# Marks of a routing table, compared on VectorE eight sets at a time instead of set by set on GpSimd

## Chip, cores and metric

One core of one Trainium2 chip runs the whole kernel. The metric is device time in microseconds from start to end of one execution; lower is better. The kernel is a single launch, so what lies between launches does not count.

## What is computed

The reference is a small transformer layer over 32 sequences of 128 tokens (4096 tokens, width 512), in float32. The first two parts (a token embedding with a low-rank correction and a norm over the whole table of 32,000 rows; an attention with quantised weights and activations) are not touched here. The third part is:

```python
h = h + ffn(layernorm(h))
# ffn(x): 8 routed experts of width 352, each token goes to its best K = 2; one shared expert of width 704
shared_out = (silu(x @ Wsg.T) * (x @ Wsu.T)) @ Wsd.T
scores = softmax(x @ Wr.T)
topk_scores, topk_idx = top_k(scores, 2)
w_full = sum over k of one_hot(topk_idx, 8) * topk_scores
out_e = (silu(x @ Wg[e].T) * (x @ Wu[e].T)) @ Wd[e].T
routed_out = sum over e of out_e * w_full[e]
return routed_out + shared_out
```

## The kernel before, in words

`experts` (line 1041 on) computes this third part. It works in blocks of 256 tokens. The first 16 blocks (kind A, numbers 0 to 15) put all tokens through one half of the shared expert; then come 39 routed blocks (32 full ones of kind B, 7 half ones of kind H), which each take the tokens of one expert; then 16 more blocks (kind C) do the other half of the shared expert. On each engine the order of the blocks is written out by hand in `each_block`: blocks 0 to 3, then a loop over blocks 4 to 11 (two per turn), then 12 to 15, and so on. The engines are coupled by semaphores alone.

One block n, in the order that each engine issues it:

- TensorE (PE) does `up_full(n)`: gate and up projections into three PSUM tiles `up_ps`, j = 0, 1, 2, each float32 product as three passes over a high and a low part (L1642 to L1644, L1671 to L1676). Then it does `down(n-1)`, the down projection of the block before, into `down_ps`. Before `up_full(n)` it waits for the low part `xT_lo` of block n; before it overwrites `up_ps` j it waits until VectorE has read tile j of block n-1 (`h_done`); before `down(n-1)` it waits for `h_lo` of block n-1.
- VectorE (DVE) does `turned_lo(n+1)`, the low part of the next block's input (L1419, 128x1024); `gate_full(n)`: for j = 0, 1, 2 the product h (L1554, and L1558 to L1565 for j = 2) and, once ScalarE has rounded it to `h_hi`, the rest `h_lo` (L1567); then `take_y(n-1)`, which adds two down results into H (L1538).
- ScalarE (ACT) rounds the next input (`xT_hi`, L1339), does silu on each `up_ps` tile (L1357 to L1361) and rounds h (L1365).
- GpSimd (POOL) is not part of a shared block. Its work in this stage is the slot table, below.

The slot table. Each of the 8192 (token, choice) pairs gets a slot, that is a place in some routed block. VectorE plans this in three pieces laid between the shared blocks: `plan_blocks` behind block 0, `plan_experts` behind block 1, `plan_slots` behind block 3 (L1486 to L1516). `plan_slots` ends with, for each of the SETS = 64 sets of 128 pairs (32 sequences times 2 choices), the slot's tile number `tile_f` (0 to 70; SLOT_TILES = 71) and its row `row_f` in that tile (0 to 127). The inverse table, which token sits in each slot, is then made by matrix products: `at_row` has a 1 where a pair's row number equals the column (128 columns a set), `at_tile` has, where the tile number equals the column (71 columns), the sequence number i in its first half and the lane number in its second. Both are bf16 in one tile `slot_marks`. TensorE's `sum_table` adds 64 products at_row x at_tile (L1637) into `route_ps`. It stands in TensorE's order between blocks 11 and 12. VectorE's `read_table` (L1522, L1524) turns the sums into the list `slot_tokens`, behind block 12 in its own order. GpSimd then gathers the rows of the routed blocks with indirect DMAs (L1316) into the buffers `xr`, the first for block 16 once `xT_lo` of block 14 is done.

The marks are made by GpSimd in a loop over the 64 sets, three instructions a set, L1302 to L1304 (see the diff); the third adds one to `slots_marked`, and `sum_table` waits for `slots_marked` set by set. GpSimd starts them when `plan_slots` has ended (semaphore `plan`). The instruction that ends `plan_slots` is L1516.

`slot_marks` lies in the space of the second weight buffer, `w_split[1]`; ScalarE writes there for the first routed block during block 15, and waits for `table_summed` before. The SyncE queue (SP) loads the tokens' rows for each shared block (two buffers, paced by `xT_lo`), and the weights of the first routed block as soon as its expert is known, before `plan_slots`.

Of the kernel before, what the change touches and what calls it, by code (L numbers as in the profile page):

```python
# [20 lines left out]
ALU = mybir.AluOpType  # L21
# [3 lines left out]
P = 128  # L25
SEQS, T = 32, 128
# [7 lines left out]
EXPERTS, TOP = 8, 2  # L34
# [1006 lines left out]
def experts(nc, packed, w_stage, x2_dram, x2T_dram, y_dram, out, H, ident, ones, gate_values, gate_experts):  # L1041
# [6 lines left out]
    with ExitStack() as ctx:  # L1048
        def sb(name, shape, dt=F32):
            return ctx.enter_context(nc.sbuf_tensor(name, shape, dt))  # L1050
# [7 lines left out]
        SETS = TOP * SEQS  # L1058
        w_split = [sb("w_split0", [P, 2 * PACKED], F32R)]

        with nc.sbuf_tensor("slot_marks", [P, SETS * (P + 2 * SLOT_TILES)], BF16) as slot_marks:
            at_row = slot_marks[:, 0:SETS * P].rearrange("p (n c) -> p n c", n=SETS)
            at_tile = slot_marks[:, SETS * P:].rearrange("p (n c) -> p n c", n=SETS)
# [26 lines left out]
        slot_i = sb("slot_i", [P, TOP * SEQS], I32)  # L1090
        lane = sb("lane", [P, 1])
        row_no = sb("row_no", [P, P])
        slot_tokens = sb("slot_tokens", [P, SLOT_TILES], I32)
        block_expert = sb("block_expert", [P, ROUTED_BLOCKS], I32)

# [33 lines left out]
        route_ps = ps("route_ps", [P, 512])  # L1129

        made, masked, plan, counted, blocks_known = sem("made"), sem("masked"), sem("plan"), sem("counted"), sem("blocks_known")
        slots_marked, table_summed, table_lo_out, table_made = sem("slots_marked"), sem("table_summed"), sem("table_lo_out"), sem("table_made")
        stage_in = [sem(f"stage_in{i}") for i in range(3)]
        w_hi_done = [sem(f"w_hi_done{i}") for i in range(3)]
        w_lo_done = [sem(f"w_lo_done{i}") for i in range(3)]
# [53 lines left out]
        def w_buffer(odd, kind):  # L1189
            return (odd + 1) % 2 if kind in ("B", "H") else 0  # L1190

        def each_block(eng, body, after_first=None, after_second=None, after_fourth=None, before_twelfth=None, after_twelfth=None):

            body(0, 0, "A", None, "A")
            if after_first:
                after_first()
            body(1, 1, "A", "A", "A")
            if after_second:
                after_second()
            body(2, 0, "A", "A", "A")  # L1200
            body(3, 1, "A", "A", "A")
            if after_fourth:
                after_fourth()
            with eng.Fori(0, (B_FROM - 8) // 2) as m:
                for u in range(2):
                    body(m * 2 + (4 + u), u, "A", "A", "A")
            if before_twelfth:
                before_twelfth()
            body(B_FROM - 4, 0, "A", "A", "A")
            if after_twelfth:  # L1210
                after_twelfth()
            body(B_FROM - 3, 1, "A", "A", "A")
            body(B_FROM - 2, 0, "A", "A", "A")
            body(B_FROM - 1, 1, "A", "A", "B")
            for n in range(B_FROM, C_FROM + 1):
                body(n, n % 2, kind_of(n), kind_of(n - 1), kind_of(n + 1))
            with eng.Fori(0, (SHARED_BLOCKS - 2) // 2) as m:
                for u in range(2):
                    body(m * 2 + (C_FROM + 1 + u), u % 2, "C", "C", "C")
            body(N - 1, 0, "C", "C", None)  # L1220
# [61 lines left out]
        def _(pool):  # L1282
# [11 lines left out]
            pool.affine_select(out=below[:, :], in_=below[:, :], compare_op=ALU.is_gt, fill=0.0, base=0, pattern=[[1, P]],  # L1294
                               channel_multiplier=-1).then_inc(masked, 1)

            pool.wait_ge(made, 6)
            pool.wait_ge(plan, 1)
            for t in range(TOP):
                for i in range(SEQS):  # L1300
                    n = t * SEQS + i
                    pool.tensor_scalar(at_row[:, n, :], row_no[:, :], row_f[:, 0, n:n + 1], None, ALU.is_equal)  # L1302
                    pool.tensor_scalar(at_tile[:, n, 0:SLOT_TILES], row_no[:, 0:SLOT_TILES], tile_f[:, 0, n:n + 1], float(i), ALU.is_equal, ALU.mult)  # L1303
                    pool.tensor_scalar(at_tile[:, n, SLOT_TILES:], row_no[:, 0:SLOT_TILES], tile_f[:, 0, n:n + 1], lane[:, 0:1],  # L1304
                                       ALU.is_equal, ALU.mult).then_inc(slots_marked, 1)
            pool.wait_ge(table_made, 1)
            for r in range(ROUTED_BLOCKS):
                n = B_FROM + r
# [106 lines left out]
        def _(dve):  # L1415
# [69 lines left out]
            def plan_slots():  # L1485
# [23 lines left out]
                for t in range(TOP):  # L1509
# [6 lines left out]
                dve.scalar_tensor_tensor(out=row_f[:, 0, :], in0=tile_f[:, 0, :], scalar=float(-P), in1=slot_f[:, 0, :],  # L1516
                                         op0=ALU.mult, op1=ALU.add).then_inc(plan, 1)

            def read_table():

                dve.wait_ge(table_summed, 1)
                dve.tensor_copy(table_lo[:, 0, :], route_ps[:, SLOT_TILES:2 * SLOT_TILES]).then_inc(table_lo_out, 1)  # L1522
                dve.wait_ge(table_lo_out, 1)
                dve.scalar_tensor_tensor(out=slot_tokens[:, :], in0=route_ps[:, 0:SLOT_TILES], scalar=float(P), in1=table_lo[:, 0, :],  # L1524
                                         op0=ALU.mult, op1=ALU.add).then_inc(table_made, 1)

# [88 lines left out]
            turned_lo(0, 0, "A")  # L1615
            weights_lo(0, 2, 0)
            plan_choices()
            each_block(dve, body, plan_blocks, plan_experts, plan_slots, None, read_table)
            take_y(N - 1, "C")
            dve.wait_ge(y_taken, 2 * N)  # L1620
            for i in range(SEQS - 2, SEQS):
# [3 lines left out]
        def _(pe):  # L1625
# [7 lines left out]
            def sum_table():  # L1633

                for n in range(SETS):
                    pe.wait_ge(slots_marked, n + 1)
                    mm = pe.matmul(route_ps[:, 0:2 * SLOT_TILES], at_row[:, n, :], at_tile[:, n, :], start=(n == 0), stop=(n == SETS - 1))  # L1637
                mm.then_inc(table_summed, 1)

# [179 lines left out]
```

## Time and profile before

| | us |
|---|---|
| median of 3 runs | 1592.19 |
| lowest and highest of them | 1588.05, 1597.53 |
| the profiled execution, its own time | 1594.22 |
| its span in the trace, first to last instruction | 1592.5 |
| mean granted TensorE clock, share of full speed | 0.979 |

The profile gives busy times of each engine, also in 40 slices of the span, so that a slice is 39.8 us. A group is a set of instructions of one line, engine and shape; behind its busy time stands the idle time of the engine just before it and what ended it. "Busy" on TensorE is modelled by the profiler, so the spacing of starts is the better measure there. The granted clock is given as a share of the higher of TensorE's two levels (2.4 GHz; 0.5 is the lower, 1.2 GHz).

### The profile page before, as it was taken

What the parts mean: (1) busy time and instruction counts of PE and PEld (TensorE: products, weight loads), DVE (VectorE), ACT (ScalarE), POOL (GpSimd) and SP (SyncE); (2) the same over time, 40 slices, a digit from 0 to 9 for tenths busy, and PEclk for the clock granted to TensorE, in tenths of its full rate; (3) what the DMA queues carried; (4) which work ended last, traced back from release to release, by engine and by line L of the source; (5) the groups of instructions that cost most, each with busy time, mean ns of one, the idle gap of its engine ahead of it and who ended that gap; (6) DMA issues with size and microseconds to landing.
All of it is one profiled execution on the core that took longest, in us unless ns stands there. A gap on an engine that the chain in (4) does not pass through costs nothing.

```text
span 1592.5 us, 36456 instructions
## 1 busy us (share of the span) xinstructions
PE 1406.5 (88%) x13322; PEld 1181.4 (74%) x13386; DVE 1175.7 (74%) x2334; ACT 909.7 (57%) x1692; POOL 551.8 (35%) x701
## 2 busy tenths in 40 slices
PE   4566875999999998699938999999999999999997
PEld 2233333777777776599918999898898898999996
DVE  5598986888888986575513777778777787767776
ACT  3787873777777776333302566666566665633331
POOL 4454545445454420019992121111111110034433
PEclk9999999999999999799968999999999999999999
DMA  8999985222222211131100477777877777443465
GB/s 305 353 327 287 329 277 108 59 72 71 68 75 65 66 41 55 67 109 52 40 14 27 152 230 270 268 241 242 282 242 265 256 236 269 168 159 126 144 209 194
DMA packets 76013, 271.45 MB, mean 170 GB/s; under 512 B 10321, under 2 KB 10833, under 8 KB 71681
## 3 DMA queue, kind: packets, MB, share of 16 engines
q1 hardware_dynamic: 59472, 226.03, 41.2%
q0 software_dynamic: 16432, 44.05, 10.9%
q8 instruction: 59, 0.97, 0.2%
q14 instruction: 50, 0.40, 0.1%
HBM read 226.27 MB, written 43.78 MB: 170 GB/s over the span
## 4 chain that ended last, share of the span: by engine, by line
PE 22%; DVE 11%; issue 8%; POOL 8%; ACT 7%; DMA 2%; SPq 0%; ACTq 0%; POOLq 0%; DVEq 0%
PE up_ps L1642 4%; PE up_ps L1644 4%; PE up_ps L1643 4%; ACT w_split L1343 3%; DVE w_split L1428 3%; POOL slot_marks L1302 3%; POOL slot_marks L1304 3%; POOL slot_marks L1303 2%; PE down_ps L1643 2%; PE down_ps L1644 2%; PE down_ps L1642 2%; DVE xT_lo L1419 2%; DVE h L1554 1%; DMA slot_rows<-y_rows 1%; PE up_ps L1676 1%
## 5 line engine op out<-in xcount | busy, mean ns | idle before, releaser
L1642 PE MATMUL up_ps<-xT_hi,w_split 128*128 128x256 f32 x1280 | 367.3, 287 | 15.2 <-DVE xT_lo L1419 8.2
L1643 PE MATMUL up_ps<-xT_lo,w_split 128*128 128x256 f32 x1280 | 363.6, 284 | 0.0
L1644 PE MATMUL up_ps<-xT_hi,w_split 128*128 128x256 f32 x1280 | 363.6, 284 | 0.0
L1642 PEld LDWEIGHTS up_ps<-xT_hi,w_split 128*128 128x128 f32 x1280 | 246.6, 193 | 18.0 <-DVE xT_lo L1419 8.3
L1643 PEld LDWEIGHTS up_ps<-xT_lo,w_split 128*128 128x128 f32 x1280 | 246.8, 193 | 1.4
L1644 PEld LDWEIGHTS up_ps<-xT_hi,w_split 128*128 128x128 f32 x1280 | 246.6, 193 | 0.0
L1365 ACT ACTIVATE h_hi<-h 128x256 fp32r<-128x256 f32 (+1 forms) x192 | 80.2, 418 | 258.2 <-DVE h L1554 195.9
L1316 POOL DMA_INDIRECT xr<-x_rows,slot_tokens x71 | 71.5, 1008 | 417.9 <-PE xT_ps L1737 381.4
L393 PE MATMUL norm_ps<-a_split,b_split 96*128 96x500 f32 x256 | 140.1, 685 | 55.9 <-DVE W L294 31.6
L294 DVE TENSOR_TENSOR W<-W,norm_ps 128x1000 f32<-128x1000 f32 x128 | 146.9, 1188 | 39.6 <-PE norm_ps L393 33.8
L1343 ACT ACTIVATE w_split<-w_stage 128x1408 fp32r<-128x1408 f32 (+1 forms) x123 | 169.1, 1411 | 3.9 <-PE down_ps L1644 1.8
L1642 PE MATMUL down_ps<-w_split,h_hi 128*128 128x512 f32 (+1 forms) x405 | 159.1, 393 | 1.5 <-DVE H L1538 1.5
L1644 PE MATMUL down_ps<-w_split,h_lo 128*128 128x512 f32 (+1 forms) x405 | 160.2, 396 | 0.0
L1643 PE MATMUL down_ps<-w_split,h_hi 128*128 128x512 f32 (+1 forms) x405 | 160.1, 395 | 0.0
L393 PEld LDWEIGHTS norm_ps<-a_split,b_split 96*128 96x128 f32 x256 | 68.4, 315 | 120.2 <-DVE W L294 82.9
L1357 ACT ACTIVATE act_g<-up_ps 128x256 f32<-128x256 f32 (+1 forms) x192 | 71.5, 372 | 140.8 <-PE up_ps L1644 122.4
L1567 DVE TENSOR_TENSOR h_lo<-h,h_hi 128x256 fp32r<-128x256 f32 (+1 forms) x192 | 82.0, 427 | 93.8 <-ACT h_hi L1365 91.4
L232 ACT ACTIVATE W<-W 128x1000 f32<-128x1000 f32 x128 | 131.3, 1026 | 32.5 <-DVE W L294 31.9
L1324 POOL DMA_INDIRECT comb<-slot_rows,slot_i x64 | 75.8, 1184 | 178.1 <-DVE H L1546 97.1
L1428 DVE TENSOR_TENSOR w_split<-w_stage,w_split 128x1280 fp32r<-128x1280 f32 x82 | 121.6, 1483 | 2.0 <-ACT w_split L1343 1.9
L186 POOL TENSOR_TENSOR a_split<-a_f,a_split 32x1000 fp32r<-32x1000 f32 x32 | 74.0, 2314 | 117.7 <-ACT a_split L224 105.5
L1554 DVE TENSOR_TENSOR h<-act_g,up_ps 128x256 f32<-128x256 f32 x128 | 53.2, 415 | 72.1 <-ACT act_g L1357 72.1
(278 smaller groups left out, 3182.4 us busy)
## 6 DMA issues: line engine op xcount, KB each, us to landing
W<-table_c SPq DMA_DIRECT2D x32, 2000.0 KB
w_stage<-packed SPq DMA_DIRECT2D x80, 704.0 KB
w_stage<-packed SPq DMA_DIRECT2D x40, 768.0 KB
xr<-x_turned SPq DMA_DIRECT2D x32, 512.0 KB
slot_rows<-y_rows SPq DMA_DIRECT2D x32, 512.0 KB
x_rows<-x SPq DMA_DIRECT2D x32, 256.0 KB, 2.0
x_turned<-x2T SPq DMA_DIRECT2D x32, 256.0 KB, 3.9
out<-H SPq DMA_DIRECT2D x32, 256.0 KB
```

What stands on the lines that cost most here:

```text
L186: pool.tensor_tensor(a_split[c % 4][64:96, :], a_f[0:32, c % 4, :], a_split[c % 4][0:32, :].bitcast(F32), ALU.subtract).then_inc(a_lo, 1)
L232: act.activation(W[:, q, k, :], W[:, q, k, :], ACT.Square, accum_out=part[:, q % 2, k:k + 1]).then_inc(squared, 1)
L294: dve.tensor_tensor(w, w, norm_ps[k % 2][:, :, 0:HALF], ALU.add).then_inc(added, 1)
L393: mm = pe.matmul(norm_ps[k % 2][:, h, 0:HALF], b_split[:, k * P:(k + 1) * P], a_split[q][:, h * HALF:(h + 1) * HALF], start=True, stop=True)
L1324: pool.indirect_dma_start(out=comb[i % 2][:, t, :], out_offset=None, in_=y_dram, in_offset=bass.IndirectOffsetOnAxis(ap=slot_i[:, t * SEQS ...
L1343: act.activation(hi_part(piece, buffer), staged(piece), ACT.Copy).then_inc(w_hi_done[piece], 1)
L1365: act.activation(h_hi[odd][0:f, j, :], h[0:f, j, :], ACT.Copy).then_inc(h_hi_done, 1)
L1428: dve.tensor_tensor(up_lo[buffer][:, k, :], whole[:, :, 0:BOTH_FROM], hi[:, :, 0:BOTH_FROM], ALU.subtract).then_inc(w_lo_done[piece], 1)
L1567: dve.tensor_tensor(h_lo[odd][0:f, j, :], h[0:f, j, :], h_hi[odd][0:f, j, :].bitcast(F32), ALU.subtract).then_inc(h_lo_done, 1)
L1642: pe.matmul(out, a_hi, b_hi, start=first, stop=False)
L1643: pe.matmul(out, a_hi, b_lo, start=False, stop=False)
L1644: return pe.matmul(out, a_lo, b_hi, start=False, stop=last)
```

## The change

The comparisons move to VectorE. `mark_slots(g)` runs ahead of block 4 + g on VectorE (g = 0 to 7, `in_loop` of `each_block`) and compares eight sets in one instruction for `at_tile` (128x568) and one for `at_row` (128x1024), both with operands that are broadcast by access pattern. GpSimd keeps two multiplications for each eight sets, 128x568 each: marks times the sequence number into the first half, marks times the lane number in place in the second half. It waits for both comparisons of the group before them, and for its own first product before the second. TensorE waits once for each eight sets. GpSimd makes one more small constant, `seq_no`. A semaphore in `read_table` is replaced by the common counter of VectorE's plan (`did`).

```diff
+        MARKED = 8
+        MARK_BLOCKS = SETS // MARKED
...
+        seq_no = sb("seq_no", [P, SETS])
...
         def each_block(eng, body, ..., in_loop=None, before_twelfth=None, after_twelfth=None):
...
-            with eng.Fori(0, (B_FROM - 8) // 2) as m:
+            with eng.Fori(0, MARK_BLOCKS // 2) as m:
                 for u in range(2):
+                    if in_loop:
+                        in_loop(m * 2 + u)
                     body(m * 2 + (4 + u), u, "A", "A", "A")
...
         # GpSimd
-            pool.wait_ge(made, 6)
-            pool.wait_ge(plan, 1)
-            for t in range(TOP):
-                for i in range(SEQS):
-                    n = t * SEQS + i
-                    pool.tensor_scalar(at_row[:, n, :], row_no[:, :], row_f[:, 0, n:n + 1], None, ALU.is_equal)
-                    pool.tensor_scalar(at_tile[:, n, 0:SLOT_TILES], row_no[:, 0:SLOT_TILES], tile_f[:, 0, n:n + 1], float(i), ALU.is_equal, ALU.mult)
-                    pool.tensor_scalar(at_tile[:, n, SLOT_TILES:], row_no[:, 0:SLOT_TILES], tile_f[:, 0, n:n + 1], lane[:, 0:1],
-                                       ALU.is_equal, ALU.mult).then_inc(slots_marked, 1)
+            pool.iota(seq_no[:, :].rearrange("p (t i) -> p t i", t=TOP), pattern=[[0, TOP], [1, SEQS]], base=0, channel_multiplier=0,
+                      allow_small_or_imprecise_dtypes=True).then_inc(made, 1)
+            pool.wait_ge(made, 7)
+            for g in range(MARK_BLOCKS):
+                n = slice(g * MARKED, (g + 1) * MARKED)
+                pool.wait_ge(slots_marked, (g + 1) * 2)
+                mark = at_tile[:, n, SLOT_TILES:]
+                pool.tensor_tensor(at_tile[:, n, 0:SLOT_TILES], mark, seq_no[:, n].unsqueeze(2).to_broadcast([P, MARKED, SLOT_TILES]),
+                                   ALU.mult).then_inc(tokens_marked, 1)
+                pool.wait_ge(tokens_marked, g * 2 + 1)
+                pool.tensor_tensor(mark, mark, lane[:, 0:1].unsqueeze(2).to_broadcast([P, MARKED, SLOT_TILES]), ALU.mult).then_inc(tokens_marked, 1)
...
         # VectorE
+            def mark_slots(g):
+                if not isinstance(g, int):
+                    dve.wait_ge(plan, 1)
+                n = bass.ds(g * MARKED, MARKED)
+                rows = row_no[:, :].unsqueeze(1)
+                dve.tensor_tensor(at_tile[:, n, SLOT_TILES:], rows[:, :, 0:SLOT_TILES].to_broadcast([P, MARKED, SLOT_TILES]),
+                                  tile_f[:, 0, n].unsqueeze(2).to_broadcast([P, MARKED, SLOT_TILES]), ALU.is_equal).then_inc(slots_marked, 1)
+                dve.tensor_tensor(at_row[:, n, :], rows.to_broadcast([P, MARKED, P]), row_f[:, 0, n].unsqueeze(2).to_broadcast([P, MARKED, P]),
+                                  ALU.is_equal).then_inc(slots_marked, 1)
...
             def read_table():
                 dve.wait_ge(table_summed, 1)
-                dve.tensor_copy(table_lo[:, 0, :], route_ps[:, SLOT_TILES:2 * SLOT_TILES]).then_inc(table_lo_out, 1)
-                dve.wait_ge(table_lo_out, 1)
+                did(dve.tensor_copy(table_lo[:, 0, :], route_ps[:, SLOT_TILES:2 * SLOT_TILES]))
...
-            each_block(dve, body, plan_blocks, plan_experts, plan_slots, None, read_table)
+            each_block(dve, body, plan_blocks, plan_experts, plan_slots, mark_slots, None, read_table)
...
         # TensorE, sum_table
                 for n in range(SETS):
-                    pe.wait_ge(slots_marked, n + 1)
+                    if n % MARKED == 0:
+                        pe.wait_ge(tokens_marked, (n // MARKED + 1) * 2)
```

## Rows read from the trace of the kernel before

**Rows 1.** The page: busy time, share of the span, instructions.

```profile
PE 1406.5 (88%) x13322; PEld 1181.4 (74%) x13386; DVE 1175.7 (74%) x2334; ACT 909.7 (57%) x1692; POOL 551.8 (35%) x701
```

**Rows 2.** The page: busy tenths and granted clock in 40 slices.

```profile
PE   4566875999999998699938999999999999999997
...
PEclk9999999999999999799968999999999999999999
```

**Rows 3.** Windows: stretch, its length, busy us of each engine, clock, DMA share, GB/s.

```profile
714.00:726.40 12.40, 12.40 (x88) 11.59 (x87) 8.99 (x20) 6.22 (x15) 11.93 (x19) 1.00 0.23 85
787.80:800.30 12.50, 12.50 (x88) 11.50 (x86) 6.73 (x14) 4.48 (x10) 11.55 (x19) 1.00 0.14 43
800.30:842.00 41.70, 9.03 (x66) 4.95 (x65) 2.25 (x3) 0.21 (x1) 37.98 (x65) 0.60 0.04 13
```

**Rows 4.** Tile slot_marks: duration ns min/median/max, first and last start, and waits.

```profile
L1302 POOL TENSOR_SCALAR slot_marks<-row_no,y_rows x64: 602/609/1615, 711.7 to 839.8; 128x128 bf16<-128x128 f32 x64
...
L1304 POOL TENSOR_SCALAR slot_marks<-row_no,y_rows,lane x64: 608/613/1252, 713.9 to 841.1; 128x71 bf16<-128x71 f32 x64
```

**Rows 5.** Timeline of PE: start us, duration us, idle before and its releaser.

```profile
701.85 0.28 PE L1642 MATMUL up_ps<-xT_hi,w_split 128*128 128x256 f32 x1
...
714.17 0.28 PE L1642 MATMUL up_ps<-xT_hi,w_split 128*128 128x256 f32 x1
...
800.36 2.90 PE L1637 MATMUL route_ps<-slot_marks 128*128 128x142 bf16 x43
...
839.85 0.30 PE L1637 MATMUL route_ps<-slot_marks 128*128 128x142 bf16 x1 [1.60 <-POOL slot_marks L1304]
...
841.96 0.55 PE L1642 MATMUL up_ps<-xT_hi,w_split 128*128 128x256 f32 x1
...
856.15 0.28 PE L1642 MATMUL up_ps<-xT_hi,w_split 128*128 128x256 f32 x1
```

**Rows 6.** Timeline of DVE, from the end of the plan on.

```profile
711.30 0.23 DVE L1516 SCALAR_TENSOR_TENSOR y_rows<-y_rows 128x64 f32<-128x64 f32 x1
711.60 1.23 DVE L1419 TENSOR_TENSOR xT_lo<-xr,xT_hi 128x1024 fp32r<-128x1024 f32 x1
712.75 0.41 DVE L1554 TENSOR_TENSOR h<-act_g,up_ps 128x256 f32<-128x256 f32 x1
...
719.75 1.22 DVE L1419 TENSOR_TENSOR xT_lo<-xr,xT_hi 128x1024 fp32r<-128x1024 f32 x1
...
779.43 0.42 DVE L1554 TENSOR_TENSOR h<-act_g,up_ps 128x256 f32<-128x256 f32 x1 [1.53 <-ACT act_g L1357]
...
789.11 1.22 DVE L1419 TENSOR_TENSOR xT_lo<-xr,xT_hi 128x1024 fp32r<-128x1024 f32 x1
```

**Rows 7.** Groups of DVE by shape: busy us, mean ns, idle before.

```profile
L1419 DVE TENSOR_TENSOR xT_lo<-xr,xT_hi 128x1024 fp32r<-128x1024 f32 x32 | 39.4, 1231 | 11.6 <-PE up_ps L1676 6.9 <-ACT xT_hi L1339 4.6
...
L1506 DVE TENSOR_TENSOR comb<-comb,y_rows 128x256 f32<-128x256 f32 x1 | 0.4, 425 | 0.0
```

**Rows 8.** Lines of POOL, its multiplications: duration ns min/median/max, first and last start.

```profile
L601 POOL TENSOR_TENSOR diag_t<-ident,dequant x32: 398/399/401, 261.2 to 603.9; 128x128 f32<-128x128 f32 x32
...
L596 POOL TENSOR_TENSOR H<-H,S_bc x32: 1263/1852/1871, 255.2 to 574.8; 128x512 f32<-128x512 f32 x32
...
L186 POOL TENSOR_TENSOR a_split<-a_f,a_split x32: 2286/2312/2343, 14.6 to 231.2; 32x1000 fp32r<-32x1000 f32 x32
```

**Rows 9.** Line 307 of DVE: duration ns min/median/max, and its register instructions.

```profile
L307 DVE TENSOR_SCALAR a_group<-a_rows x8: 242/780/1835, 31.1 to 232.2; 128x128 f32<-128x128 f32 x4, 128x128 f32 x4
L307 DVEq FUSED_REGOPS  x4: 65/65/65, 152.9 to 230.9; - x4
```

**Rows 10.** Timelines of POOL and DVE where a long POOL product meets L307.

```profile
29.36 2.29 POOL L186 TENSOR_TENSOR a_split<-a_f,a_split 32x1000 fp32r<-32x1000 f32 x1 [0.42 <-ACT a_split L224]
...
31.05 0.68 DVE L307 TENSOR_SCALAR a_group<-a_rows 128x128 f32<-128x128 f32 x1 [2.65 <-DMA a_rows<-lora_a_t,rows_i]
```

More of the change, by code:

```diff
@@ L1131, in experts @@
         made, masked, plan, counted, blocks_known = sem("made"), sem("masked"), sem("plan"), sem("counted"), sem("blocks_known")
-        slots_marked, table_summed, table_lo_out, table_made = sem("slots_marked"), sem("table_summed"), sem("table_lo_out"), sem("table_made")
+        slots_marked, tokens_marked, table_summed, table_made = sem("slots_marked"), sem("tokens_marked"), sem("table_summed"), sem("table_made")
         stage_in = [sem(f"stage_in{i}") for i in range(3)]
@@ L1190, in w_buffer, with each_block @@
             return (odd + 1) % 2 if kind in ("B", "H") else 0
-        def each_block(eng, body, after_first=None, after_second=None, after_fourth=None, before_twelfth=None, after_twelfth=None):
+        def each_block(eng, body, after_first=None, after_second=None, after_fourth=None, in_loop=None, before_twelfth=None, after_twelfth=None):
             body(0, 0, "A", None, "A")
```

## Prediction

> **What bounds the kernel now.** I read the totals first. TensorE is busy for 88% of the span, VectorE for 74%, GpSimd for 35% [rows 1]: GpSimd looks harmless. The 40 slices say where TensorE is not busy. After its slow first stage it stands at 9 almost everywhere, except in slices 17 and 21 (counted from 1), and the granted clock falls in the same two [rows 2]. Slice 21 is 796 to 836 us. The windows around it show what happens [rows 3]: until 800.3 us TensorE has no idle time at full clock, then for 41.7 us it is busy for 9.0, at a mean clock of 0.60, while GpSimd is busy for 38.0 of them and VectorE, ScalarE and DMA do almost nothing (DMA share 0.04).
>
> The tile that GpSimd works on is `slot_marks`: 64 sets of three instructions, from 711.7 us to 841.1 [rows 4]. It cannot start earlier, since the plan ends at 711.5 [rows 6]. TensorE comes to `sum_table` at 800.36, finds 43 sets ready and takes them in 2.90 us, and then waits for GpSimd set by set, one each 1.90 us, until block 12 begins at 841.96 [rows 5]. So in this stage GpSimd ends last, and in the shared blocks before it TensorE does. One block takes TensorE 714.17 - 701.85 = 12.32 us [rows 5].
>
> **What is removed.** Of the 41.60 us between 800.36 and 841.96 the 64 products themselves remain. The 43 ready ones took 2.90 us including a tail of about 0.2 for the last one to drain, so 0.064 us each, 4.1 us for 64. That leaves 41.6 - 4.1 = **37.5 us** of waiting. There is a second part. Block 12 takes from 841.96 to 856.15 [rows 5], 14.19 us where another takes 12.32: the mean clock in the wait was 0.60 and block 12 starts at the lower one. Without the wait the clock should stay at 1.00, as in both full blocks of [rows 3]: **1.9 us** more.
>
> **What is added on VectorE.** Both comparisons read two SBUF operands and are float32 in. The nearest rows are float32 `tensor_tensor` instructions: 1024 elements in 1.231 us (1.22 when nothing disturbs, as at 789.11 in [rows 6]) and, with a broadcast second operand, 256 in 0.425 [rows 7]. The line through them is 1.04 ns an element and 0.16 fixed. That makes 1.22 us for `at_row` and 0.16 + 568 x 1.04 ns = 0.75 for `at_tile`, together **1.97 us a block** and 15.8 in all. The bf16 output and the broadcast of both operands have no row of their own; I take the plain rate since the broadcast in L1506 cost nothing.
>
> Is it on the path? VectorE needs 719.75 - 711.60 = 8.15 us for a block when it waits for nothing but ScalarE's roundings [rows 6], and TensorE needs 12.32. So there is room for about 4.2 us a block, and in the settled blocks VectorE waits 1.5 us for silu at tile 0 alone (the row at 779.43 in [rows 6]) and is busy for 6.7 of 12.5 [rows 3]. Work of 1.97 fits there, and there I cost it at nothing; what hides it is TensorE's own 12.32. If VectorE's block passed that, each further us would cost a us, eight times.
>
> It does not fit in block 4. VectorE comes out of the plan late: its `turned_lo(5)` starts at 711.60 and the product for tile 0 of block 4 ends at 712.75 + 0.41 = 713.16, and TensorE needs both for block 5, which it begins at 714.17 [rows 5, 6]. The slack is 1.0 us. `mark_slots(0)` stands ahead of both: 1.97, plus a wait for the plan's last instruction and a few register instructions for the moving slices, at 0.065 each [rows 9], about 0.3 together. TensorE then stands for 2.3 - 1.0 = **1.3 us**, once. The other conditions have more room (low part of h and tile 2 are over 2 us early), and after that VectorE gains on TensorE by 12.3 - 10.4 = 1.9 a block, so block 6 is no longer late.
>
> **What is left on GpSimd.** Two multiplications of 568 elements for each group. Its products have rows at 128, 512 and 1000 elements: 0.399, 1.263 at least, 2.312 [rows 8]; by a straight line 568 take 1.39 us. Two are 2.8 us in each block of 12.3. The pessimistic end is L596's median, 1.852 for 512, which gives some 2.05 us each. The last group is marked ahead of block 11, on VectorE around 791 us, so GpSimd is done at 795 to 797, and TensorE asks at 800.4 + 1.3. The margin is at least 4 us, and TensorE's 8 waits in `sum_table` cost nothing. The new `seq_no` is one short constant before the plan, in a time when GpSimd is idle. `read_table` does the same work with another semaphore: nothing.
>
> **GpSimd against VectorE.** A long GpSimd product can hold VectorE up. In [rows 10] L186 runs from 29.36 to 31.65; L307 on VectorE starts at 31.05 and ends at 31.73, 0.68 us for work that takes 0.242 alone, and its longest is 1.835 [rows 9]. In the stage at hand L1302's longest is 1.615 against a median of 0.609 [rows 4], so it goes the other way too. Before the change GpSimd's instructions were short; now they are 1.4 us long. What VectorE may lose is at most the two products, 2.8 us a block, part of it in gaps where it waits for ScalarE anyhow. I expect about 1 us a block, hidden from block 5 on, and nothing at block 4's critical start, because `turned_lo` is issued directly behind the comparison that GpSimd waits for. The bounds: 0, and 1.4 us at the start plus (8.15 + 2.3 + 2.8 - 12.3) = 0.95 in each of the seven later blocks, 8 us.
>
> The Trainium skill (SBUF — State Buffer, section "Who interferes with whom") speaks against the change here: it says that a VectorE instruction with two SBUF inputs and a GpSimd instruction that reads SBUF exclude each other, and that the one that comes second blocks until the first has ended. Taken literally every comparison, L1419 and L1567 could wait for a full product, which is the upper bound just named and the first rival below. The trace agrees in the form of [rows 10].
>
> **The sum.** Removed: 37.5 + 1.9 = 39.4. Added: 1.3. Net 38.1. Against the profiled execution's own time, 1594.2 - 38.1 = 1556.1. That execution lies 2.0 above the median of the three runs, so for the median I say 1592.2 - 38.1 = **1554.1 us**. What follows block 12 moves as a whole: nothing is loaded during the stall that a later stage lives on (DMA share 0.04), and the gathers for the routed blocks wait for `xT_lo` of block 14, which moves along.
>
> **Rivals.**
>
> 1. *GpSimd's products block VectorE for their whole length, block after block.* For it: [rows 9, 10]. Against it: VectorE's block has gaps, and its products with PSUM operands are most of the rest. The gain shrinks by up to 8 us: 1554 + 8 = 1562. Faster still. Chance 0.13.
> 2. *The wait comes back in another place.* VectorE reaches the mark ahead of block 11 late, or GpSimd's products run much slower on bf16 operands with two broadcasts, so that TensorE waits in `sum_table` for the last groups. It decides when GpSimd needs more than 12.3 us a group, 4.4 times what I price. At 17 us a group it would end at 712 + 8 x 17 = 848, 6 us later than now: about 1592 + 6 - 4 = 1594, no change. Chance 0.02.
> 3. *Slower: the comparisons run at a slow rate and VectorE bounds blocks 4 to 11.* The place is `mark_slots`; the price is the slowest rate that the trace has for VectorE, L307's longest, 1.835 us for 128 elements [rows 9], 14 ns an element; that is 23 us for 1592 elements, at half that 11.4. The point from which it decides against the change: 8 x (8.15 + m - 12.3) > 38, that is m over 8.9 us a block, 4.5 times my price. At m = 11.4 it costs 8 x 7.25 = 58 and the kernel ends near 1612. Against it: L1506, a broadcast at full rate. Chance 0.03.
> 4. *The change doesn't do what it says*: the start of the routed blocks is held by something else that the stall hid, such as the first gathers, and the gain is given back in part. The nearest thing is the idle DMA in [rows 3], which speaks against it. Half of the 38 would leave 1573. Chance 0.04.
>
> The forecast itself has 0.78.
>
> **How the numbers follow.** Three runs of the kernel before span 1588 to 1598, so the best case is 39.4 gained without the stall at block 5 and 5 for the runs: 1548. The other end is rival 1 with 8 us and 4 for the runs: 1566. That leaves out rivals 2 to 4 and some tails. About 0.5% (8 us) is what a measurement of this kernel can tell from no change. Faster by more than that: forecast, rival 1 and rival 4, 0.95. Within it: rival 2, 0.02. Slower: rival 3, 0.03.
>
> **What the profile of the changed kernel would show.** `sum_table` as one run of 64 products in about 4 us, near 801.7, with no GpSimd behind it as releaser, and block 12 near 806 at clock 1.00. Two comparisons in each of eight blocks on VectorE, 0.75 and 1.22. One idle stretch of TensorE of 1.3 us before block 5, released by `xT_lo` or h. GpSimd with 16 products of 1.4 us. L1419 and L1567 longer than 1.22 and 0.42 in these blocks would show the blocking; idle time of TensorE at several blocks with VectorE as releaser would make rival 1 or 3 true. I am wrong if the time is outside 1548 to 1566, or if the stages before 700 or after 870 change their length.

## The result, and the profile of the changed kernel

| | before | changed |
|---|---|---|
| median of the runs, us | 1593.41 (4 runs) | 1555.70 (4 runs, 1555.41 to 1556.17) |
| ratio, 95% interval | | 0.9765 (0.9743 to 0.9786) |
| span of the profiled execution, us | 1592.5 | 1553.7 |
| mean granted clock | 0.979 | 0.991 |

The change is worth 37.7 us, 2.4%, and the median of 1555.70 stands against a forecast of 1554.1 us. That forecast was 38.1 below 1592.19, the median of the kernel before over three runs; with a fourth run it is 1593.41. The page's totals and two of the slices lines, which answer to [rows 1, 2]:

```profile
PE 1400.4 (90%) x13322; PEld 1179.3 (76%) x13386; DVE 1189.6 (77%) x2350; ACT 909.8 (59%) x1692; POOL 456.1 (29%) x526
...
PE   4576775999999999599999999999999999999997
...
PEclk9999999999999999699999999999999999999999
```

GpSimd has 95.7 us less, VectorE 13.9 more, and of the two dips of TensorE and its clock only the first is left. (VectorE's new work is 8 x (0.744 + 1.218) = 15.7 us by the rows below; the profile doesn't say where it saves the other 1.8.) The tile `slot_marks` answers to [rows 4]; columns as there:

```profile
L1534 DVE TENSOR_TENSOR slot_marks<-row_no,y_rows x8: 742/744/751, 711.9 to 790.3; 128x568 f32 x8
L1536 DVE TENSOR_TENSOR slot_marks<-row_no,y_rows x8: 1216/1218/1219, 712.6 to 791.0; 128x1024 f32 x8
L1311 POOL TENSOR_TENSOR slot_marks<-slot_marks,seq_no x8: 1978/2057/2061, 714.0 to 792.3; 128x568 bf16<-128x568 bf16 x8
L1314 POOL TENSOR_TENSOR slot_marks<-slot_marks,lane x8: 1191/1217/1242, 716.0 to 794.4; 128x568 bf16<-128x568 bf16 x8
```

The last marks are ready at 794.4 + 1.2 = 795.6, six us before TensorE asks. TensorE's timeline around the stage, against [rows 5] (start, duration, idle before and its releaser):

```profile
715.34 0.39 PE L1662 MATMUL up_ps<-xT_hi,w_split 128*128 128x256 f32 x1 [0.95 <-DVE h L1573]
...
801.65 4.24 PE L1657 MATMUL route_ps<-slot_marks 128*128 128x142 bf16 x64
805.69 0.36 PE L1662 MATMUL up_ps<-xT_hi,w_split 128*128 128x256 f32 x1
...
818.09 0.28 PE L1662 MATMUL up_ps<-xT_hi,w_split 128*128 128x256 f32 x1
```

All 64 products now run as one piece of 4.04 us where 41.60 us passed before. Between 700 and 870 us there is one idle stretch left, before block 5, released by VectorE's product h.

**How the runs below are compared.** The runs of the kernel before spread over 1588 to 1602 us on several chips, and their median moved with the chip (1591.9 beside e1 to e4, 1599.3 beside e5 to e7, 1596.1 beside e8 and e9), so a difference of 1 or 2 us doesn't show in the times. It shows in the spacing: the time from the start of one block's first projection to the next is 12.31 to 12.32 us whenever TensorE waits for nothing. The table gives it for each profile, worked out from the starts in TensorE's timeline; e1 to e9 are the runs described below, in order.

| us | block 4 | block 5 | blocks 6 to 11 | sum, start of block 4 to `sum_table` |
|---|---|---|---|---|
| before | 12.32 | 12.31 | 12.31 to 12.32 | 98.51 |
| changed | 13.42 | 12.42 | 12.31 to 12.32 | 99.73 |
| e1 | 12.31 | 12.31 | 12.31 to 12.32 | 98.51 |
| e2 | 16.85 | 13.91 | 12.99, 13.52, 13.37, 13.53, 13.36, 12.43 | 109.96 |
| e3 | 17.41 | 13.87 | 12.57, 13.33, 13.14, 13.33, 13.14, 12.42 | 109.21 |
| e4 | 12.31 | 12.32 | 12.31 to 12.32 | 98.51 |
| e5 | 14.98 | 13.86 | 12.31 to 12.32 | 102.73 |
| e6 | 13.38 | 12.42 | 12.31 to 12.32 | 99.68 |
| e7 | 15.19 | 13.90 | 12.31 to 12.32 | 102.98 |
| e8 | 13.55 | 12.41 | 12.31 to 12.32 | 99.84 |
| e9 | 12.32 | 12.31 | 12.31 to 12.32 | 98.51 |

### The profile page after: what moved, and what is told of

Its sections match the earlier page's. It is cut to its first block, busy times and chain, and to the rows that moved or that the text cites. A ratio compares the mean times of both kernels' runs of the same rounds, so it can differ in the third digit from the quotient of the medians.

```text
span 1553.7 us, 36325 instructions
## 1 busy us (share of the span) xinstructions
PE 1400.4 (90%) x13322; PEld 1179.3 (76%) x13386; DVE 1189.6 (77%) x2350; ACT 909.8 (59%) x1692; POOL 456.1 (29%) x526
## 4 chain that ended last, share of the span: by engine, by line
PE 28%; DVE 11%; issue 6%; ACT 6%; DMA 5%; SPq 0%; ACTq 0%; POOL 0%; DVEq 0%; POOLq 0%
PE up_ps L1662 6%; PE up_ps L1664 5%; PE up_ps L1663 5%; PE down_ps L1663 3%; PE down_ps L1664 3%; PE down_ps L1662 3%; DVE w_split L1437 3%; ACT w_split L1352 3%; DMA slot_rows<-y_rows 3%; DVE xT_lo L1428 2%; DMA w_stage<-packed 2%; DVE h L1573 1%; PE up_ps L1696 1%; DVE w_split L1434 1%; PE up_ps L1691 1%
## 5 line engine op out<-in xcount | busy, mean ns | idle before, releaser
L1586 DVE TENSOR_TENSOR h_lo<-h,h_hi 128x256 fp32r<-128x256 f32 (+1 forms) x192 | 81.6, 425 | 93.8 <-ACT h_hi L1374 93.8
L1434 DVE TENSOR_TENSOR w_split<-w_stage,w_split 128x1536 fp32r<-128x1536 f32 x41 | 72.1, 1758 | 33.5 <-ACT w_split L1352 33.3
```

Of the source, the lines that this page charges most:

```text
L1434: dve.tensor_tensor(down_lo[buffer], whole, hi, ALU.subtract).then_inc(w_lo_done[piece], 1)
L1586: dve.tensor_tensor(h_lo[odd][0:f, j, :], h[0:f, j, :], h_hi[odd][0:f, j, :].bitcast(F32), ALU.subtract).then_inc(h_lo_done, 1)
```

## Experiments

**e1: the marks behind the first product.** The theory is that the one new wait is not the work's but its place in VectorE's order. The marks move behind the product for tile 0:

```diff
-            each_block(dve, body, plan_blocks, plan_experts, plan_slots, mark_slots, None, read_table)
+            each_block(dve, body, plan_blocks, plan_experts, plan_slots, held.append, None, read_table)
...
             # gate_full, j < 2, behind the product h
+                        if held:
+                            mark_slots(held.pop())
```

> The marks of a block are made behind VectorE's product for tile 0 of that block, not ahead of its turned_lo. Theory (the idle stretch before block 5 is the delay of turned_lo and of the first product): block 5 begins at 714.2 with no idle time before it, against 715.3 in the changed kernel, sum_table at about 800.4, and the time is 1.1 us lower, 1554.6. Rival (the work itself costs wherever it stands, since VectorE is late out of the plan): TensorE stands by about as much at another place of block 5 (tile 1, or the down projection waiting for take_y), and the time stays at 1555.7.

Measured: 1553.88 us (5 runs, 1552.88 to 1559.98), ratio 0.9768 (0.9749 to 0.9787). TensorE has no idle time between 700 and 800 us; block 4 is 12.31, where the changed kernel has 13.42. The mechanism is as expected. The absolute place is not: `sum_table` starts at 801.68 and not at 800.4, because this execution comes to block 4 at 703.17, 1.25 us later than the changed kernel's (701.92). That is scatter of the stages before, and a reason to read spacings.

This run showed something else. VectorE's timeline in block 7, and below it GpSimd's:

```profile
746.47 0.42 DVE L1575 TENSOR_TENSOR h<-act_g,up_ps 128x256 f32<-128x256 f32 x1 [0.33 <-ACT act_g L1366]
747.38 1.26 DVE L1590 TENSOR_TENSOR h_lo<-h,h_hi 128x256 fp32r<-128x256 f32 x1 [0.48 <-ACT h_hi L1374]
```

```profile
745.89 1.26 POOL L1311 TENSOR_TENSOR slot_marks<-slot_marks,seq_no 128x568 bf16<-128x568 bf16 x1 [8.56 <-DVE slot_marks L1536]
747.22 1.13 POOL L1314 TENSOR_TENSOR slot_marks<-slot_marks,lane 128x568 bf16<-128x568 bf16 x1
```

L1590 needs 0.42 us alone. Here it starts 0.16 behind GpSimd's second product and takes 1.26: it ends 0.29 after the product does. This happens in five of the eight blocks, from block 7 on (1.26 to 1.31 us each). In the changed kernel the same instruction never takes over 0.466 us. e6 takes that up.

**e2: three times the comparisons.** How much room has VectorE? Two more pairs a block, into the tiles `comb`, which are free in this stage:

```diff
             # mark_slots, ahead of its two comparisons
+                for c in comb[:2]:
+                    spare = c[:, :, :].rearrange("p t d -> p (t d)").bitcast(BF16)
+                    dve.tensor_tensor(spare[:, MARKED * P:MARKED * (P + SLOT_TILES)].rearrange("p (n c) -> p n c", n=MARKED),
+                                      rows[:, :, 0:SLOT_TILES].to_broadcast([P, MARKED, SLOT_TILES]),
+                                      tile_f[:, 0, n].unsqueeze(2).to_broadcast([P, MARKED, SLOT_TILES]), ALU.is_equal)
+                    dve.tensor_tensor(spare[:, 0:MARKED * P].rearrange("p (n c) -> p n c", n=MARKED), rows.to_broadcast([P, MARKED, P]),
+                                      row_f[:, 0, n].unsqueeze(2).to_broadcast([P, MARKED, P]), ALU.is_equal)
```

> Two more pairs of the same comparisons ahead of each block, into space that is free there: about 3.8 us more on VectorE in each of the eight blocks. Theory (a block has room for some 4.2 us on VectorE, and what goes past it costs one for one): VectorE needs 7.9 + 5.7 = 13.6 us a block where TensorE needs 12.3, so TensorE stands 4.9 us before block 5 and 1.3 to 1.4 before each of the next seven: 13.5 us more than the changed kernel, about 1569. Rival (no such bound, the work hides in waits): only the first block's delay, 3.8, 1559.5. Rival (GpSimd's products block VectorE, more so when it is full): L1586 and L1428 longer than 0.47 and 1.25, time over 1573.

Measured: 1566.30 us (4 runs, 1564.89 to 1568.08), ratio 0.9837 (0.9822 to 0.9852). The waits of TensorE between 680 and 900 us:

```profile
PE up_ps L1669 <- DVE h L1580: 8.4, 6, 4.4
```

Six waits, as a VectorE-bound stretch gives: one of 4.4 before block 5 and five of 0.5 to 0.9 before blocks 7 to 11, and settled blocks of 13.4 to 13.5 us. The theory holds: past 12.31 us on VectorE, each us costs one. VectorE's block in the changed kernel, before it settles, is 9.8 to 9.9 us (GpSimd's first products, each behind a group's comparisons, start at 723.83, 733.60 and 743.53), and two more pairs of 1.79, from start to start, make 13.4, as measured. The size was 10 to 11 us over the changed kernel (10.2 by the spacing) and not 13.5, since a pair costs 1.79 and not 1.9, and since the marks ahead of block 11 delay nothing (the block behind it comes after `sum_table`). Block 5 is different from the others: no wait stands behind it, and its 13.91 us are those of the lower clock (granted 0.61 over the first 3.0 us after the wait of 4.4 us, 0.50 over the next one). L1593 (`h_lo`) stayed at a mean of 0.446, so GpSimd did not get in the way here.

**e3: one set at a time, on VectorE.** Is it the engine or the batch? The lines are shortened: how the outputs are viewed, the waits, the semaphore that TensorE waits for and the removal of GpSimd's two products are left out.

```diff
             # mark_slots, in place of the two comparisons of eight sets
+                for k in range(MARKED):
+                    n = bass.ds(g * MARKED + k, 1)
+                    dve.tensor_scalar(at_row[:, n, :], row_no, row_f[:, 0, n], None, ALU.is_equal)
+                    dve.tensor_scalar(at_tile[:, n, 0:SLOT_TILES], row_no[:, 0:SLOT_TILES], tile_f[:, 0, n], seq_no[:, n], ALU.is_equal, ALU.mult)
+                    dve.tensor_scalar(at_tile[:, n, SLOT_TILES:], row_no[:, 0:SLOT_TILES], tile_f[:, 0, n], lane[:, 0:1], ALU.is_equal, ALU.mult)
```

> VectorE makes the marks one set at a time with three instructions as GpSimd did in the kernel before, 24 a block; GpSimd makes none. Theory (it is the eight sets to an instruction that make it fit): each takes 0.22 to 0.28 us, 5.9 us a block, 13.8 with the rest, over TensorE's 12.3: about 5 us before block 5 and 1.5 before each later one, 1570. Rival (the engine is what matters, one or eight sets are alike): 24 instructions in about 2 us, time within 2 us of 1555.7.

Measured: 1566.41 us (4 runs, 1563.54 to 1569.08), ratio 0.9845 (0.9830 to 0.9860). The tile's rows:

```profile
L1525 DVE TENSOR_SCALAR slot_marks<-row_no,y_rows x64: 274/281/299, 710.6 to 808.4; 128x128 f32 x64
L1526 DVE TENSOR_SCALAR slot_marks<-row_no,y_rows,seq_no x64: 310/318/334, 710.9 to 808.6; 128x71 f32 x64
L1528 DVE TENSOR_SCALAR slot_marks<-row_no,y_rows,lane x64: 306/314/331, 711.1 to 808.8; 128x71 f32 x64
```

Settled blocks are 13.1 to 13.3 us, the middle of the stage is bound by VectorE, and 9.5 us of the gain by the spacing (10.7 by the medians) are given back. Block 5 has no wait behind it here either; it pays for the lower clock after a wait of 4.9 us. So the batch matters: three small instructions pass in 0.65 us a set, 5.2 us a block, for the marks that two comparisons with 1.8 us of VectorE and two products of GpSimd make. This run changes two things against the changed kernel, the batch and the place of the multiplications. e7, which has all marks on VectorE in batches of eight, separates them: from e7 to e3 the stage grows by 109.21 - 102.98 = 6.2 us, and that is the batch. But moved to VectorE without any batch the change would still have won 25 of the 38 us by the medians (28.6 by the spacing), since VectorE had most of the room.

**e4: the comparisons back on GpSimd, its multiplications batched.**

```diff
             # GpSimd, ahead of the two multiplications of the group; VectorE makes no marks (the waits are left out)
-                pool.wait_ge(slots_marked, (g + 1) * 2)
+                for k in range(g * MARKED, (g + 1) * MARKED):
+                    pool.tensor_scalar(at_row[:, k, :], row_no[:, :], row_f[:, 0, k:k + 1], None, ALU.is_equal)
+                    pool.tensor_scalar(at_tile[:, k, SLOT_TILES:], row_no[:, 0:SLOT_TILES], tile_f[:, 0, k:k + 1], None, ALU.is_equal)
```

> The comparisons go back to GpSimd, one set at a time with two instructions, and the two multiplications for eight sets stay. VectorE makes no marks. Theory (GpSimd's fixed price an instruction bounds it, so a third fewer instructions give back part of the wait): 64 x 1.29 + 8 x 2.3 = 101 us alone, some 9% more beside VectorE, so GpSimd ends near 818 to 821, TensorE waits from 800.4 to then at a falling clock, and the time is 1569 to 1574. Rival (the multiplications of eight cost GpSimd as much as before): as the kernel before, 1593. No idle time before block 5 in any case.

Measured: 1564.12 us (4 runs, 1562.33 to 1566.13), ratio 0.9828 (0.9812 to 0.9843), faster than either theory said. The rows of the tile, and TensorE:

```profile
L1311 POOL TENSOR_SCALAR slot_marks<-row_no,y_rows x64: 591/597/1685, 711.7 to 808.4; 128x128 bf16<-128x128 f32 x64
L1312 POOL TENSOR_SCALAR slot_marks<-row_no,y_rows x64: 460/464/710, 713.3 to 808.9; 128x71 bf16<-128x71 f32 x64
L1314 POOL TENSOR_TENSOR slot_marks<-slot_marks,seq_no x8: 1139/1140/1242, 723.2 to 809.5; 128x568 bf16<-128x568 bf16 x8
L1317 POOL TENSOR_TENSOR slot_marks<-slot_marks,lane x8: 1134/1135/1138, 724.5 to 810.7; 128x568 bf16<-128x568 bf16 x8
```

```profile
800.44 3.73 PE L1660 MATMUL route_ps<-slot_marks 128*128 128x142 bf16 x56
811.89 1.13 PE L1660 MATMUL route_ps<-slot_marks 128*128 128x142 bf16 x8 [7.72 <-POOL slot_marks L1317]
812.77 0.56 PE L1665 MATMUL up_ps<-xT_hi,w_split 128*128 128x256 f32 x1
```

A comparison of 71 elements without a multiplication behind it takes 0.464 us on GpSimd, against 0.613 with one [rows 4]; my price of 1.29 us a set took the old spacing over. The two products took 1.14 us each, so the 2.3 for both was right. GpSimd ends at 811.8 instead of 818 to 821. With no help from VectorE, 28 of the 38 us are there by the medians (30 by the spacing, up to the start of block 13): eight sets take 16 instructions, of which 8 are lighter than before, and 2 large ones, where they took 24. What is left against the changed kernel is 7.7 us of waiting, 1.3 of clock behind it (0.4 in the last eight products, which take 0.88 where eight take 0.5 at the full clock, and 0.9 in block 12, which takes 13.30 against 12.40) and 0.2 in which the products before the wait drain, less the 1.2 that the changed kernel loses in blocks 4 and 5. That is what the move of the comparisons to VectorE adds, together with their being made for eight sets at once: no run makes them eight at a time on GpSimd, so the two are not separated.

**e5: twice the comparisons.** As e2, but with one extra pair a block in place of two.

> One more pair of the same comparisons ahead of each block, 1.9 us. Theory (room up to TensorE's 12.3 us, then one for one): VectorE needs 9.85 + 1.9 = 11.8 us a block, still under 12.3, so only the first delay grows, by 1.9 to about 3.0 us before block 5, and nothing stands before the later blocks: sum_table 1.9 us later than in the changed kernel, time about 1557.6. Rival (cost in proportion, a third of what the run with three pairs paid over the changed kernel per pair, 10.6 / 2): 1561.

Measured: 1560.04 us (4 runs, 1557.63 to 1563.12), ratio 0.9759 (0.9737 to 0.9782), where the runs before had a median of 1599.29. Against the changed kernel the stage is 102.73 - 99.73 = 3.0 us longer, all of it in blocks 4 and 5; from block 6 on, none. The median lies nearer to the rival's 1561 than to the theory's 1557.6, but the rival puts a cost into every block, and the spacing shows none from block 6 on. So the bound is as the theory has it, but 1.9 were expected. TensorE's wait is 2.50 us, so block 4 accounts for 1.6 of the 3.0. The other 1.4 stand in block 5, where TensorE waits for nothing. The windows (stretch, its length, busy us of each engine, clock, DMA share, GB/s):

```profile
712.60:715.09 2.49, 0.01 (x1) 0.01 (x1) 2.43 (x3) 0.00 (x0) 1.37 (x1) 0.98 0.00 0
715.09:718.00 2.91, 2.91 (x13) 2.91 (x14) 1.27 (x3) 1.75 (x5) 1.85 (x2) 0.50 0.50 179
718.00:719.00 1.00, 1.00 (x9) 1.00 (x8) 0.85 (x3) 0.41 (x1) 0.00 (x0) 0.80 0.03 12
719.00:720.00 1.00, 1.00 (x11) 1.00 (x10) 0.82 (x2) 0.12 (x1) 0.00 (x0) 1.00 0.00 0
```

After 2.5 us of idling TensorE ran at 0.50, its 1.2 GHz level, for some 3 us, and block 5 took 13.86 us instead of 12.31. The changed kernel's stretch of 0.95 us had no such price, in its own windows:

```profile
714.30:715.30 1.00, 0.09 (x1) 0.00 (x0) 0.98 (x2) 0.00 (x0) 1.00 (x1) 1.00 0.00 0
715.34:718.00 2.66, 2.66 (x22) 2.66 (x23) 1.25 (x4) 1.75 (x5) 1.85 (x2) 1.00 0.58 189
```

**e6: five more products on GpSimd.** This is for the question that e1 raised.

```diff
             # GpSimd, behind the two multiplications of the group (each waits for the one before it; the waits are left out)
+                for k in range(5):
+                    pool.tensor_tensor(spare[:, :, :], mark, seq_no[:, n].unsqueeze(2).to_broadcast([P, MARKED, SLOT_TILES]), ALU.mult)
```

> GpSimd makes five more products of 128x568 a group behind the two real ones, into a spare tile, so that it is busy for some 9 of 12.3 us in blocks 4 to 11. Theory (a GpSimd product and a VectorE instruction with two SBUF inputs exclude each other): the mean of L1586 over these blocks rises from 0.43 to 0.6 us or more with single ones over 1.2, L1584 too, while L1573 with a PSUM input stays at 0.41; VectorE's block grows from 9.85 to some 12 us, which is about what TensorE needs, so the time is 1556 to 1560. Rival (they do not touch, VectorE's ops only looked unhindered in the changed kernel because they are): L1586 stays at 0.43 and the time at 1555.7.

Measured: 1556.19 us (4 runs, 1554.63 to 1561.35), ratio 0.9738 (0.9711 to 0.9765), and the same spacings as the changed kernel. VectorE in a block in the middle:

```profile
740.62 0.42 DVE L1587 TENSOR_TENSOR h<-act_g,up_ps 64x256 f32<-64x256 f32 x1
741.08 0.72 DVE L1590 TENSOR_TENSOR h<-act_g,h 32x256 f32<-32x256 f32 x1
742.29 0.79 DVE L1592 TENSOR_TENSOR h_lo<-h,h_hi 96x256 fp32r<-96x256 f32 x1 [0.48 <-ACT h_hi L1380]
743.11 1.28 DVE L1563 TENSOR_TENSOR H<-H,down_ps 128x512 f32 x2
744.31 1.59 DVE L1540 TENSOR_TENSOR slot_marks<-row_no,y_rows 128x568 f32 x1
```

The instructions with two SBUF operands that start well inside one of GpSimd's products are longer: 0.72 for 0.42 (0.72 to 0.84 in seven blocks, 1.38 in the last), 0.79 to 0.80 for 0.42 in all eight, and the comparison 1.59 for 0.74 in the seven blocks where a product is under way at its start. Those with an operand in PSUM are not: over the whole execution L1579 stays within 0.423.

```profile
L1579 DVE TENSOR_TENSOR h<-act_g,up_ps x128: 406/414/423, 658.4 to 1531.8; 128x256 f32<-128x256 f32 x128
```

The exclusion is shown, and the starts and ends in the timelines of VectorE and GpSimd give its size. A VectorE instruction with two SBUF operands that starts while a product is under way takes its own time plus what is left of the product, less 0.14 us. Where the product has more than those 0.14 us left, this holds to 0.01 us for every such meeting in e1 and e6: in e1's block 7, 0.42 + 0.98 - 0.14 = 1.26. The same sum holds the other way, for GpSimd, which needs 1.14 us alone. In the changed kernel's block 5 (VectorE, then GpSimd):

```profile
723.66 1.22 DVE L1428 TENSOR_TENSOR xT_lo<-xr,xT_hi 128x1024 fp32r<-128x1024 f32 x1
725.70 0.47 DVE L1586 TENSOR_TENSOR h_lo<-h,h_hi 128x256 fp32r<-128x256 f32 x1 [0.48 <-ACT h_hi L1374]
```

```profile
723.83 2.06 POOL L1311 TENSOR_TENSOR slot_marks<-slot_marks,seq_no 128x568 bf16<-128x568 bf16 x1 [6.56 <-DVE slot_marks L1536]
725.97 1.19 POOL L1314 TENSOR_TENSOR slot_marks<-slot_marks,lane 128x568 bf16<-128x568 bf16 x1
```

The product starts with 1.05 us of `turned_lo` left and takes 1.14 + 1.05 - 0.14 = 2.05. `h_lo` starts with 0.19 us of the product left and takes 0.47. Where the exclusion strikes was expected in part: the mean of the 128x256 `h_lo` was 0.446, not 0.6, because it always met the last 0.1 to 0.2 us of a product, as in the changed kernel; L1590's longest was 1.384. VectorE still had room, and nothing reached TensorE.

**e7: the multiplications on VectorE too.**

```diff
             # mark_slots, behind the comparisons; GpSimd makes none (the waits are left out)
+                dve.tensor_tensor(at_tile[:, n, 0:SLOT_TILES], mark, seq_no[:, n].unsqueeze(2).to_broadcast([P, MARKED, SLOT_TILES]), ALU.mult)
+                dve.tensor_tensor(mark, mark, lane[:, 0:1].unsqueeze(2).to_broadcast([P, MARKED, SLOT_TILES]), ALU.mult)
```

> VectorE makes the two multiplications too, GpSimd nothing: 0.75 us each by the rate of the comparisons, so 1.6 with its waits. Theory: VectorE's block is 11.4 us, under 12.3, the delay before block 5 grows from 1.1 to 2.7, nothing else; time 1557.3, and sum_table still without a wait. Rival (what the change gains hangs on sharing the work between two engines): TensorE stands before several blocks and the time is over 1562.

Measured: 1561.21 us (4 runs, 1560.72 to 1561.79), ratio 0.9760 (0.9740 to 0.9780). The stage is 3.25 us longer than the changed kernel's, 1.8 in block 4 and, as in e5, 1.5 in block 5 at the lower clock level (the windows, columns as in e5):

```profile
716.16:718.87 2.71, 0.00 (x1) 0.00 (x1) 2.62 (x4) 0.00 (x0) 0.00 (x0) 1.00 0.01 3
718.87:721.00 2.13, 2.13 (x10) 2.13 (x11) 1.14 (x3) 1.47 (x5) 0.00 (x0) 0.52 0.53 173
721.00:722.00 1.00, 1.00 (x7) 1.00 (x7) 0.54 (x3) 0.34 (x2) 0.00 (x0) 0.50 0.41 156
```

No block after it is longer, so the theory's bound holds, though the median lies nearer to the rival's 1562. On the same chip e6, which has the spacings of the changed kernel, took 1556.19 us: e5 is 3.9 and e7 5.0 above it, more than the 3.0 and 3.25 of the stage, by less than the runs of e6 spread. By the spacing GpSimd's part in the changed kernel is worth about 3 us, and half of that is clock.

**e8 and e9: the changed kernel and e1's on one chip.**

> The changed kernel itself, beside the next one on the same chip. 38 us under the kernel before, ratio 0.976; TensorE's idle stretch of 0.9 to 1.0 us before block 5 and a block of 13.4 us there, at clock 1.00 after it.

> The marks behind the product for tile 0, once more, beside the changed kernel. Theory: no idle stretch, all blocks 4 to 11 12.31 to 12.32 us, median 1.1 us under the changed kernel's on the same chip, as far as the spread of the runs lets that be seen. Rival: the difference of 1.8 us between the medians seen before was between chips, and the two are alike to within 0.3.

Measured: 1558.17 us (5 runs, 1554.38 to 1559.01) and 1555.44 us (6 runs, 1552.68 to 1560.13); ratios to the kernel before 0.9747 (0.9723 to 0.9772) and 0.9741 (0.9717 to 0.9765). The changed kernel is 37.9 us under the kernel before again. The medians lie the right way, but the runs overlap and the intervals do too: by the times the two can't be told apart. By the profiles they can. TensorE waited 1.08 us in e8 and at no place of blocks 4 to 11 in e9, and the stage takes 99.84 and 98.51 us. Version e9 is the best that I have, by 1.2 to 1.3 us of the trace; with all blocks at 12.31 and the 64 products at 4.04 us nothing is left to gain on TensorE between block 4 and block 12 by moving marks about.

## Why the prediction was right, point by point

- *The wait, 37.5 us.* Measured 41.60 - 4.04 = 37.56. It was the time from TensorE's arrival to block 12, less the products alone, both in [rows 5].
- *The clock, 1.9 us.* Block 12 took 14.19 us and now takes 818.09 - 805.69 = 12.40: 1.8. (The 0.1 over a block of 12.31 stands in every run whose block 12 starts at the full clock.)
- *The comparisons, 0.75 and 1.22 us.* Measured medians 0.744 and 1.218. The line through plain float32 rows carried over to broadcasts of both operands and a bf16 output.
- *The stand before block 5, 1.3 us.* Measured 13.42 - 12.31 = 1.11, with 0.1 more in the next block. The slack of 1.0 was about right; the two comparisons pass in 1.80 us (711.93 to 713.73, where `turned_lo` starts), not in the 1.97 that their durations add up to. e1 and e9 show that the place of the marks makes it: behind the first product it is gone.
- *Nothing in the later blocks, room of 4.2 us.* All are 12.31 to 12.32. e5 (3.6 us of marks, no cost from block 6 on) and e2 (5.4, 1.1 us a block) bracket the room.
- *GpSimd's products, 1.39 us, done at 795 to 797.* They take 1.14 us with nothing in the way (e4), so the line through the longer float32 rows was 0.25 too high, and 2.06 and 1.22 in the changed kernel. They were done at 795.6.
- *GpSimd against VectorE, about 1 us a block, hidden.* This step was wrong in size for the changed kernel. VectorE lost next to nothing, since L1586 there never took more than 0.466 us. GpSimd lost instead: its first product takes 2.06 us, because `turned_lo` starts just before it, and each product had all but ended (0.1 to 0.2 us left) when VectorE's next instruction with two SBUF operands began. That is luck of the order; e1 and e6 show VectorE held for 0.8 us with the products in other places. The Trainium skill (SBUF — State Buffer, section "Who interferes with whom") says that whichever comes second is blocked until the first has ended; e1's 1.26 us agrees. The upper bound I drew from it was not reached, because it takes every meeting at its worst: VectorE's instructions with a PSUM operand go free, and the others came at the end of a product. And the trace that I called in agreement, [rows 10], was another form: L307 is a `tensor_scalar` with one SBUF tensor as input. That it waited for GpSimd's product is so, but the form with two inputs is shown by e1 and e6 alone.
- *The sum.* At the start of block 13 the changed kernel is 856.15 - 818.09 = 38.06 us ahead, against 38.1 forecast. The spans differ by 38.8; the other 0.7 us lies behind the start of block 13, and its cause is open. The net came out right although it was made of small misses that cancel: the clock 0.1 less, the stand with what follows it 0.1 less.

**The rivals.** The first (blocking for whole products, up to 8 us) exists as a mechanism (e1, e6) and cost nothing. The second (GpSimd too slow for `sum_table`) missed by six us of margin; the 4 us taken off in its price have no row. The third (VectorE as the bound) did not occur, as the comparisons ran at the plain rate, but e2 and e3 bring its mechanism about with 5.2 to 5.4 us of marks a block. Its formula, 8 x (8.15 + m - 12.3), gives 10 us at m = 5.4, and e2's stage is 11.5 us longer than an unhindered one. The total is near, the places are not: 4.5 us in block 4, 1.6 in block 5 by the clock, and 5.3 in the six blocks behind it. Its 58 us belong to m = 11.4, which no run comes near. The fourth, something else that the stall hid, did not appear.

**What I left out.** An idle stretch of TensorE has a second price. For 1.3 us there was none, so the forecast did not suffer. But I expected e5 and e7 at +1.9 and +1.6 us, and they came out at +3.0 and +3.25, since a stretch of 2.5 to 2.7 us brought the lower clock level with it. That the stand of 1.3 us would have no such price was taken for granted in the working, without a row for it, and that much is luck.

## What to carry to other kernels

Read a stage's bound where an engine comes to a wait and where it leaves it: an engine that is busy for 35% of the kernel held all others up for 37 us. Before moving work to another engine, count its instructions: taking the multiplications out of 64 sets and doing them for eight at a time was worth 28 of 38 us (30 by the spacing) without any move (e4), and whether the move cost anything was decided by the room that VectorE had in a block (12.3 less 8.1 us). The first block behind a late engine has less room than the others, so put added work behind what the next engine waits for, not ahead of it.

## What the runs showed of the hardware

- TensorE idle for 0.95 us went on at clock 1.00; idle for 2.5 us (e5) and 2.7 us (e7) it went on at 0.50 for about 3 us, which cost 1.5 us each time. Longer waits cost about the same: 1.6 us in block 5 after 4.4 (e2) and 4.9 us (e3), 1.3 after 7.7 us (e4: 0.4 in the last products, 0.9 in block 12), 1.8 after the 37.6 us of the kernel before.
- A GpSimd product and a VectorE instruction with two SBUF operands exclude each other in both directions: GpSimd 2.06 for 1.14 us behind a `turned_lo`, VectorE 1.26 for 0.42 behind a product. The second takes its own time plus what is left of the first less 0.14 us (e1, e6, the changed kernel), so the same pair of instructions costs VectorE 0.05 us or 0.84, by where it meets. With a PSUM operand VectorE was not held (0.423 at most over 128), nor did it hold a product (1.13 to 1.14 us in e6).
- GpSimd's instructions on 71 to 128 elements took 0.46 to 0.61 us, and products of 568 elements 1.14 (e4): eight sets in one cost as much as two or three single ones.
